# Decoder layer in fp16 pieces: the cross-attention mask is written into the score bank by ScalarE instead of multiplied in by TensorE or added by VectorE

## The reference

```
q = rope((x @ wq)), k = rope((ctx @ wk)), v = ctx @ wv       # per group: 4 query heads, 1 key/value head
scores = einsum('bhgqd,bhkd->bhgqk', q, k) / sqrt(128)
masked = where(mask[:, None, None].astype(bool), scores, -1e9)   # mask: (8, 128, 128), one per sequence
w = softmax(masked); out = einsum('bhgqk,bhkd->bhgqd', w, v) @ wo
x = layernorm(x + out)
```

## Time and profile before

| | |
|---|---|
| median of 3 runs | 884.78 us |
| profiled execution, first to last instruction (span) | 882.2 us |
| TensorE busy | 842.7 us (96%) |
| VectorE busy | 718.1 us (81%) |
| GpSimd busy | 601.9 us (68%) |
| ScalarE busy | 497.2 us (56%) |
| mean granted TensorE clock | 0.991 |
| chain that ended last, by engine | TensorE 47%, GpSimd 18%, VectorE 14%, ScalarE 9%, issue 8%, DMA 4% |
| first and last identity product with the mask | 215.3 us, 716.1 us |

### The profile page before, as it was taken

How to read it: one execution, slowest core, us unless ns; L and a number is a source line. 1 busy time by engine, 2 the same in 40 slices (tenths; PEclk the granted TensorE clock), 3 DMA queues, 4 the chain that set the end, 5 groups by cost and what they waited for, 6 DMA issues and landing times.

```text
span 882.2 us, 17330 instructions
## 1 busy us (share of the span) xinstructions
PE 842.7 (96%) x6141; PEld 471.2 (53%) x6141; DVE 718.1 (81%) x1121; ACT 497.2 (56%) x1487; POOL 601.9 (68%) x534
## 2 busy tenths in 40 slices
PE   9899999999899999999999999999999799999997
PEld 4667777655455555554555555555555444333443
DVE  5598898887787888699788788797899564899897
ACT  5788888543555555565565565555555552777400
POOL 1265959896666776677677567578888542887895
PEclk9999999999999999999999999999999899999999
DMA  6765245103124412414225125124431322230011
GB/s 178 231 208 171 64 148 162 53 17 104 37 78 139 108 37 73 108 38 133 56 33 150 38 44 148 25 55 114 85 91 25 90 41 74 90 121 18 1 48 48
DMA packets 119893, 76.75 MB, mean 87 GB/s; under 512 B 72861, under 2 KB 104064, under 8 KB 119808
## 3 DMA queue, kind: packets, MB, share of 16 engines
q1 hardware_dynamic: 117504, 74.99, 31.6%
q10 hardware_dynamic: 2304, 0.66, 0.3%
HBM read 52.50 MB, written 6.36 MB: 67 GB/s over the span
## 4 chain that ended last, share of the span: by engine, by line
PE 47%; POOL 18%; DVE 14%; ACT 9%; issue 8%; DMA 4%; SPq 0%; ACTq 0%; POOLq 0%; DVEq 0%
PE bank L361 13%; PE bank L362 12%; PE bank L363 12%; POOL rot L640 3%; ACT prob L957 2%; DVE total L1316 2%; ACT prob L817 2%; POOL q2l L646 2%; POOL pn L657 2%; DVE rsin L1180 1%; POOL xqs L589 1%; POOL deq L669 1%; POOL xql L593 1%; POOL left L673 1%; DMA pT<-pn 1%
## 5 line engine op out<-in xcount | busy, mean ns | idle before, releaser
L650 POOL TENSOR_TENSOR prob<-prob,rden 128x512 f32<-128x512 f32 x64 | 66.6, 1041 | 129.1 <-DVE rden L1245 129.1
L640 POOL TENSOR_TENSOR rot<-rcos,rsin 128x512 f32<-128x512 f32 x80 | 106.6, 1333 | 14.3 <-DVE rsin L1180 14.2
L361 PE MATMUL bank<-aTh,xqh 128*128 128x512 f16 x256 | 97.0, 379 | 2.1 <-DVE aTl L1070 1.1
L361 PE MATMUL bank<-xoh,o2h 128*128 128x512 f16 x256 | 97.8, 382 | 0.0
L362 PE MATMUL bank<-xol,o2h 128*128 128x512 f16 x256 | 97.8, 382 | 0.0
L363 PE MATMUL bank<-xoh,o2l 128*128 128x512 f16 x256 | 97.6, 381 | 0.0
L363 PE MATMUL bank<-aTh,xql 128*128 128x512 f16 x256 | 97.0, 379 | 0.0
L362 PE MATMUL bank<-aTl,xqh 128*128 128x512 f16 x256 | 97.0, 379 | 0.0
L957 ACT ACTIVATE prob<-bank,ebias 128x128 f32<-128x128 f32 x256 | 90.6, 366 | 2.1
L1180 DVE SCALAR_TENSOR_TENSOR rsin<-bank,sinq 64x512 f32<-64x512 f32 x128 | 88.1, 688 | 1.7
L646 POOL TENSOR_TENSOR q2l<-rot,q2h 128x512 f16<-128x512 f32 x64 | 82.2, 1285 | 4.4 <-ACT q2h L853 4.4
(11 more groups left out here) (215 smaller groups left out, 2632.7 us busy)
## 6 DMA issues: line engine op xcount, KB each, us to landing
tst<-tables SPq DMA_DIRECT2D x11, 768.0 KB, 5.7
xqs<-in_xwq SPq DMA_DIRECT2D x8, 1024.0 KB, 7.0
xos<-in_xwo SPq DMA_DIRECT2D x8, 1024.0 KB, 5.7
qst<-in_fq SPq DMA_DIRECT2D x11, 384.0 KB, 3.5
kstk<-stack SPq DMA_DIRECT2D x48, 64.0 KB, 2.3
qstk<-stack SPq DMA_DIRECT2D x21, 128.0 KB, 2.6
xs<-in_ctxT SPq DMA_DIRECT2D x2, 1024.0 KB, 7.7
res<-in_x SPq DMA_DIRECT2D x1, 2048.0 KB, 8.7
```

The lines of the kernel that those rows point to most:

```text
L361: pe.matmul(out_ap, ah, bh, start=first, stop=False)
L640: nc.gpsimd.tensor_tensor(rot[:, r % 2, :], rcos[:, r % 2, :], rsin[:, r % 2, :], ALU.add).then_inc(rope_rot, 1)
L650: nc.gpsimd.tensor_tensor(prob[:, v % 2, :].rearrange("p (h k) -> p h k", h=QH), prob[:, v % 2, :].rearrange("p (h k) -> p h k", h=QH), rd ...
```

## The change

`scores(v)` issues no mask product in any step, and VectorE adds no mask in any step. ScalarE has a new instruction per step, `seed_mask(v)`: it copies the mask of the sequence, repeated four times, from SBUF into the whole score bank `2 + v % 2` as float32. All 12 score products then accumulate on what is there (none of them starts a bank). `seed_mask(v + 2)` stands directly behind `exps(v)` in ScalarE's program, since `exps(v)` is the last reader of that bank; the first two stand behind the exponentials of the last two self-attention steps. TensorE's waits for the mask and for the exponentials are replaced by one wait for the seed.

```diff
-def masked_late(v):
-
-    return sum(1 for f in fills_at(T0 + v) if FILLS[f][1] in "kvq") == 2
-
-
-MASKED_LATE = [v for v in range(STEPS) if masked_late(v)]
...
+            def seed_mask(v):
+                if v < 2:
+                    act.wait_ge(mask_ready, 1)
+                    act.wait_ge(exp_done, STEPS1 - 1 + v)
+                else:
+                    act.wait_ge(c_exp, v - 1)
+                nc.scalar.copy(bank[2 + v % 2][:, :].rearrange("p (h k) -> p h k", h=QH),
+                               mbias[:, batch_of(v), :].unsqueeze(1).to_broadcast([P, QH, S])).then_inc(c_seeded, 1)
+
...
                 if 0 <= t < STEPS1:
                     exps1(t)
+                if t >= STEPS1 - 2 and t < STEPS1:
+                    seed_mask(t - STEPS1 + 2)
                 if 1 <= t <= STEPS1:
                     p1_hi(t - 1)
...
                 if v < STEPS:
                     exps(v)
+                if v + 2 < STEPS:
+                    seed_mask(v + 2)
                 rotations(fills_at(t - 1)[1:])
...
-                if v in MASKED_LATE:
-                    full = bank[2 + v % 2][:, :].rearrange("p (h k) -> p h k", h=QH)
-                    if v == MASKED_LATE[0]:
-                        dve.wait_ge(mask_ready, 1)
-                    nc.vector.tensor_tensor(full, full, mbias[:, batch_of(v), :].unsqueeze(1).to_broadcast([P, QH, S]),
-                                            ALU.add).then_inc(c_masked, 1)
-                    dve.wait_ge(c_masked, MASKED_LATE.index(v) + 1)
...
-                if v == 0:
-                    pe.wait_ge(mask_ready, 1)
-                if v < 2:
-                    pe.wait_ge(exp_done, STEPS1 - 1 + v)
-                else:
-                    pe.wait_ge(c_exp, v - 1)
-                full = bank[2 + v % 2]
-                late = v in MASKED_LATE
-                if not late:
-                    pe_.matmul(full[:, :].rearrange("p (h k) -> p h k", h=QH), identb[:, :],
-                               mbias[:, b, :].unsqueeze(1).to_broadcast([P, QH, S]), start=True, stop=False)
+                pe.wait_ge(c_seeded, v + 1)
+                onto_mask = dict(skip_group_check=True)
                 for h in range(QH):
-                    dst = full[:, h * S:(h + 1) * S]
-                    pe_.matmul(dst, q2h[:, n % 2, h, t], k2h[:, n % 2, t], start=late, stop=False)
...
+                    dst = bank[2 + v % 2][:, h * S:(h + 1) * S]
+                    pe_.matmul(dst, q2h[:, n % 2, h, t], k2h[:, n % 2, t], start=False, stop=False, **onto_mask)
```

More of the change, by code:

```diff
@@ L340, in decoder_kernel @@
         v2_hi = sem("v2_hi")
-        c_masked = sem("c_masked")
+        c_seeded = sem("c_seeded")
         c_s, c_nmax, c_ebias, c_exp = sem("c_s"), sem("c_nmax"), sem("c_ebias"), sem("c_exp")
@@ L1642, in scores @@
                 n = v // BH
-                b, t = batch_of(v), slice(v % BH * S, (v % BH + 1) * S)
+                t = slice(v % BH * S, (v % BH + 1) * S)
                 if v % BH == 0:
                     pe.wait_ge(rope_lo, 1 + max(ropes_before(f) for f in ROPES if FILLS[f][2][0] == n))
-                if v == 0:
-                    pe.wait_ge(mask_ready, 1)
-                if v < 2:
-                    pe.wait_ge(exp_done, STEPS1 - 1 + v)
-                else:
-                    pe.wait_ge(c_exp, v - 1)
-                full = bank[2 + v % 2]
-                late = v in MASKED_LATE
-                if not late:
-                    pe_.matmul(full[:, :].rearrange("p (h k) -> p h k", h=QH), identb[:, :],
-                               mbias[:, b, :].unsqueeze(1).to_broadcast([P, QH, S]), start=True, stop=False)
-                for h in range(QH):
-                    dst = full[:, h * S:(h + 1) * S]
-                    pe_.matmul(dst, q2h[:, n % 2, h, t], k2h[:, n % 2, t], start=late, stop=False)
-                    pe_.matmul(dst, q2h[:, n % 2, h, t], k2l[:, n % 2, t], start=False, stop=False)
-                    last = pe_.matmul(dst, q2l[:, n % 2, h, t], k2h[:, n % 2, t], start=False,
-                                      stop=(late or h == QH - 1))
+                pe.wait_ge(c_seeded, v + 1)
+                onto_mask = dict(skip_group_check=True)
+                for h in range(QH):
+                    dst = bank[2 + v % 2][:, h * S:(h + 1) * S]
+                    pe_.matmul(dst, q2h[:, n % 2, h, t], k2h[:, n % 2, t], start=False, stop=False, **onto_mask)
+                    pe_.matmul(dst, q2h[:, n % 2, h, t], k2l[:, n % 2, t], start=False, stop=False, **onto_mask)
+                    last = pe_.matmul(dst, q2l[:, n % 2, h, t], k2h[:, n % 2, t], start=False, stop=(h == QH - 1), **onto_mask)
                 last.then_inc(c_s, 1)
```

## The result

| | before | after |
|---|---|---|
| median of 20 runs each | 884.16 us | 885.21 us |
| ratio, 95% interval | | 1.0016 [1.0009, 1.0023] |
| span of the profiled execution | 882.2 us | 883.6 us |
| granted TensorE clock, mean over the runs (before: over those of the comparisons below) | 0.991 to 0.992 | 0.986 |

The account below looks back on a forecast made before the run. TensorE's own work bounds steps 4 to 46; elsewhere chains through VectorE, ScalarE and GpSimd do. 0.45 + 0.1 - 4.3 + 0.3 - 0.5 + 0.9 + 0.1 = -2.95 us gave 881.8 us, range 878.0 to 884.8.

Parts of the forecast that it names:

- Price of the seed: Each of 64 ScalarE copies into a bank takes 0.52 us, 33 us in all; unknown between 0.48 and 0.70.
- Step 1: End of self-attention, 199 to 207 us: step 0's seed delays `pT` and the chain to `v2l`; +0.45 us.
- Step 2: Steps 0 to 3: products 0 to 2 save nothing, step 3's saves 0.43, a seed delays 0.5; +0.1 us.
- Step 3: Steps 5 to 44: twenty products at 0.216 us saved on busy TensorE, seeds fit into ScalarE's waits; -4.3 us.
- Step 4: Steps 45 to 50: VectorE is behind on projection weights, a seed passes through, step 48's product saves 0.2; +0.3 us.
- Step 5: 613.6 to 665 us: VectorE finishes 0.3 us earlier at TensorE's 652.69 wait, step 56's product gives 0.2; -0.5 us.
- Step 6: 665 to 692 us: GpSimd, VectorE and ScalarE chain; seeds cost 0.4 in step 56, 0.5 in 59; +0.9 us.
- Step 7: 692 to 722 us: two products save 0.43, the seed behind `exps(61)` delays the chain by 0.5; +0.1 us.
- Behind it nothing is changed: Behind the wait at 721.59 us, to the end of the run: no gain or loss counted.
- B: Rival, chance 0.16: gains and costs cancel, by 0.9 us bank writes on seven path seeds or accumulating ScalarE lateness; 884.5 us.
- A: Rival, chance 0.16: TensorE's saving arrives nearly whole and VectorE's backlogs at 587 and 653 us vanish; 875.8 or 877.3 us.
- C: Rival, chance 0.08: slower through the seed's length, from 0.94 us per seed; at 1.4 us, 888.0 us.

Follow-up runs that it names:

- e7: Against the kernel before: seeds for steps 5 to 44 only, behind `exps`, all other steps keeping product or addition; 879.86 us, ratio 0.9949.
- e8: Kernel before, no seeds, plus identity products that nobody reads in TensorE's three longest waits (steps 2 and 59); 882.32 us, ratio 0.9977.
- e17: Changed kernel with one seed, the one behind `exps(56)`, moved to the end of ScalarE's step; 884.01 us, ratio to the kernel before 0.9998.
- e13: Changed kernel with one seed, the one behind `exps(61)`, moved to the end of ScalarE's step; 883.35 us, ratio to the kernel before 0.9984.
- e15: Kernel before with one seed replacing step 63's identity product, between `wdh` and `pn` of ScalarE's step 61; 883.33 us, ratio 0.9987.
- e11: Changed kernel with the seeds behind `exps(0)` to `exps(50)` moved to the end of the step; 883.32 us, ratio to the kernel before 0.9990.
- e4: Changed kernel with seeds only for the 37 identity products; VectorE keeps its 27 additions; 886.91 us, ratio to the kernel before 1.0034.
- e9: Changed kernel with the five seeds behind `exps(51)` to `exps(55)` moved to the end of the step; 884.15 us, ratio to the kernel before 0.9994.
- e14: Changed kernel with one seed, the one behind `exps(53)`, moved to the end of the step; 885.17 us, ratio to the kernel before 1.0014.
- e16: Changed kernel with one seed, the one behind `exps(52)`, moved to the end of the step; 885.02 us, ratio to the kernel before 1.0006.
- e5: Changed kernel with all seeds moved to the very end of ScalarE's step; 878.56 us, ratio to the kernel before 0.9934.
- e2: Changed kernel with the mask left out: no product, no addition, no seed; 879.04 us, ratio to the kernel before 0.9941.
- e18: Changed kernel with three seeds, behind `exps(52)`, `exps(56)` and `exps(61)`, moved to the end of the step; 881.78 us, ratio to the kernel before 0.9969.
- e10: Changed kernel with the six seeds behind `exps(56)` to `exps(61)` moved to the end of the step; 881.80 us, ratio to the kernel before 0.9966.
- e12: Changed kernel, 62 seeds at the step's end, steps 3 and 60 keeping their product, plus unread products in TensorE's waits; 876.33 us, ratio to the kernel before 0.9908.

## Why the prediction was wrong

Point by point, by the steps of the prediction; the differences are those of the two profiled executions.

- **What bounds it.** Right: two regimes, and e7 shows that the first gives its whole saving (0.9949, 4.5 us). Also right that chains through the other engines decide behind 587 us. What was missed: a chain through VectorE and GpSimd has no fixed length.
- **Price of the seed.** Right, 0.51 us against 0.52. The factor of about three that the Trainium skill gives in ScalarE: Activation LUTs, section Rules for kernel authors, is for bf16 instructions with one source, and it did not carry over: 0.51 us for the seed against 0.70 for VectorE's addition. The 0.48 us worked out from the Trainium skill's Perfetto Trace Analysis, section Optimizing Scalar/DVE Operations, was near, and the rows stood nearer.
- **In time for TensorE.** Right, no wait for a seed anywhere.
- **Step 1**, end of self-attention: +0.45 forecast, +0.67 in the trace (from +0.71 at 200 us to +1.38 at the first fill), with the forecast wait of TensorE for `v2l`, 0.54 us.
- **Step 2**, steps 0 to 3: +0.1 forecast, +0.16 (to +1.54 at 246 us).
- **Step 3**, steps 5 to 44: -4.3 forecast, -4.0. The 0.3 is a wait for the DMA of the probabilities that grew from 0.14 to 0.45 us at 390 us. It is not shown to be the seeds' doing: e8, which has none, waits 0.47 us there, and e7, which has those of steps 5 to 44, does not.
- **Step 4**, steps 45 to 50: +0.3 forecast, -0.2: the wait at 585 us grew by 0.07 only.
- **Step 5**, 613.6 to 665: -0.5 forecast, +0.65. This is the first term that failed. "0.7 less for step 54's addition, 0.4 more for a seed" took VectorE's work as a sum. The missing addition gave VectorE nothing there. The piece behind it, `xol`, started 2.5 us ahead of the kernel before and took 2.60 instead of 1.87 us; it ends 0.54 us behind GpSimd's `deq` before and 0.55 us behind it with the change. And the seed behind `exps(52)` cost 0.51 plus 0.61 us. The two pairs, before and changed:
```profile
646.98 3.09 POOL L669 TENSOR_TENSOR deq<-dif,tst 128x1536 f32<-128x1536 f16 x1 [0.89 <-DVE dif L1300]
...
648.75 1.87 DVE L1070 SCALAR_TENSOR_TENSOR xol<-xos,xoh 128x512 f16<-128x512 f32 x1
```
```profile
645.18 3.10 POOL L661 TENSOR_TENSOR deq<-dif,tst 128x1536 f32<-128x1536 f16 x1 [0.89 <-DVE dif L1298]
...
646.22 2.60 DVE L1075 SCALAR_TENSOR_TENSOR xol<-xos,xoh 128x512 f16<-128x512 f32 x1
```
- **Step 6**, 665 to 692: +0.9 forecast, +1.8. The seed in step 56 "takes back 0.4"; in the traces it costs 1.23 us (the wait at 686 us is 3.70 with it and 2.47 in e17), by the times 1.6 us with an uncertainty of about 1.
- **Step 7**, 692 to 722: +0.1 forecast, +0.3. The seed behind `exps(61)` did cost its 0.5 here; what the forecast had no word for is that `wdl` was already blocked by `pn` in the kernel before, which a seed some 2 us later in the same step undoes (e13, e15).
- **"Behind it nothing is changed"**: 0 forecast, +1.3. From 722 to 725 us, at the half clock, TensorE falls back by 1.7 us, and 0.35 of it is made up by 756 us. This was the second kind of failure: a longer wait of TensorE was priced at its length alone. The stretch is not in every execution: of six other profiles with a wait of 2.3 to 2.4 us there, one shows it (e11, not e4, e9, e14, e16, e17). But the mean clock of all runs is 0.986 against 0.992. From e8, where 0.005 more clock went with 2.0 us, this is worth some 2 us, an estimate. By the same estimate about half of it is there with the seeds in a better place or left out too: e5 has a clock of 0.989, e2 of 0.988.

The failed terms make 1.15 + 0.9 + 0.2 + 1.3 = 3.6 us, the others and the 0.71 us of the start another 0.8: from -2.95 to +1.4.

Of the rivals, B came nearest in its time (884.5), but not by its mechanism: the seed is not longer, and lateness of one-fill steps did not add up. A is true of another kernel: with the seeds at the end of the step the saving arrives (e5). C's condition, 0.94 us per seed, was never met by the seed's length, yet three seeds did cost 0.9 to 2.8 us each (the 0.9 of e16 is within the noise, but its wait at 651 us is shorter by 1.04); the mistake was to look for a long seed instead of at what stands behind it. The trace of the kernel before has a row that tells it: `wdl` takes 1.64 us at 636.77, 2.4 times an undisturbed one.

Open: what makes the seeds up to step 50 cost 2.3 us together (e11), where the terms of steps 1 to 4 give less than 1. Of the 7.3 us, the 3.1 that the three seeds of e18 leave are not traced to single seeds. The group from 56 on leaves no such rest: e13 and e17 make 4.4 us together, as much as e10.

## What to carry to other kernels

Put work that nobody waits for behind the pieces that others do wait for, at the point where its engine itself waits next; the same 64 copies cost 6.6 us directly behind the exponentials and nothing on balance at the end of the step. Where a piece feeds a VectorE operation with both inputs in SBUF, look at which GpSimd operation starts around it: here a start 0.07 us behind GpSimd's made 1.64 us out of 0.68. And a wait of TensorE like those of 2.3 to 4.1 us here is to be priced with the clock behind it, in some executions at least; the best version here (e12, 876.3 us, 0.9908) takes some 2.3 us of its 8.1 from products that nobody reads.

## What was not expected of the hardware

- VectorE's 128 x 512 subtraction with both inputs in SBUF takes 0.68 us or 1.64 us, by whether GpSimd's operation started 0.07 us ahead of it or 0.45 us behind it. A blocked one ended 0.54 or 0.55 us behind the end of GpSimd's instruction, in all 62 cases of over 1.1 us of the two kernels; 0.51 us of extra work on ScalarE, ahead of GpSimd's operation, made the kernel 1.1 us faster (e15).
- ScalarE's copy of a broadcast bf16 mask into a whole bank as float32 takes 0.58 us, 0.51 from start to start, against 0.70 us for VectorE's addition in the bank.
- Thirty products that nobody reads, in waits of 1.8 to 4.1 us, raise the mean granted clock from 0.992 to 0.997 and shorten the run by 0.23% [0.14, 0.32].
